# One core's decoder stack: five edits at the start of the attention, in its block order, at its end and in the first FFN block

## The reference, cut to what matters

```python
x = x + layernorm(attention(layernorm(x), Wqkv, Wo))      # 32 heads of 16, one shared key and value head,
                                                          # causal, slope * (k - q) added to the scores
x = x + layernorm(ffn(layernorm(x), 4-bit gate/up/down))  # h = silu(x @ Wg) * (x @ Wu);  out = h @ Wd, width 1376
x = x + layernorm(block-masked linear(layernorm(x)))
x = x + layernorm(linear + low-rank Fourier update(layernorm(x)))
# dequantisation: W[k, n] = scale[group(k), n] * (code[k, n] - (zero[group(k), n] + 1))
```

## Time and profile before

| | |
|---|---|
| three runs, median (lowest, highest) | 1154.56 us (1153.49, 1155.82) |
| the profiled execution | 1155.38 us |
| its span on the core | 1153.6 us |
| TensorE busy | 1095.1 us (95%) |
| VectorE, ScalarE, GpSimd busy | 717.3, 624.1, 423.1 us |
| mean granted TensorE clock | 0.986 |

### The profile page before, as it was taken

How to read it: one execution, slowest core, us unless ns; L and a number is a source line. 1 busy time by engine, 2 the same in 40 slices (tenths; PEclk the granted TensorE clock), 3 DMA queues, 4 the chain that set the end, 5 groups by cost and what they waited for, 6 DMA issues and landing times.

```text
span 1153.6 us, 16292 instructions
## 1 busy us (share of the span) xinstructions
PE 1095.1 (95%) x5822; PEld 678.7 (59%) x5888; DVE 717.3 (62%) x1675; ACT 624.1 (54%) x1067; POOL 423.1 (37%) x494
## 2 busy tenths in 40 slices
PE   7699999999999999899998899999999999999997
PEld 7445346345334334334535667788878878777885
DVE  6597997996999999799622644251141151247674
ACT  5265875766778689987794434211111111136775
POOL 4364252354210634322265655221121121124765
PEclk8799999999999999999999999999999999999999
DMA  6416104003213012101310221330030032211101
GB/s 184 131 43 166 29 20 119 21 20 77 62 38 101 22 35 64 58 29 47 95 37 28 75 64 39 110 110 1 1 110 1 1 79 101 74 37 74 37 37 74
DMA packets 66349, 70.62 MB, mean 61 GB/s; under 512 B 39854, under 2 KB 45510, under 8 KB 64708
## 3 DMA queue, kind: packets, MB, share of 16 engines
q1 hardware_dynamic: 62540, 59.82, 17.4%
q0 software_dynamic: 3152, 8.63, 2.3%
q10 hardware_dynamic: 576, 1.11, 0.3%
HBM read 50.27 MB, written 18.87 MB: 60 GB/s over the span
## 4 chain that ended last, share of the span: by engine, by line
PE 78%; DVE 11%; ACT 5%; issue 2%; POOL 2%; DMA 1%; SPq 1%; POOLq 0%; DVEq 0%; ACTq 0%
PE PO L1511 10%; PE ST L1497 8%; PE bank L1413 8%; PE f_pair L61 7%; PE f_pair L63 7%; PE f_pair L62 7%; DVE bank L1207 3%; PE f_Y L1906 3%; PE f_Y L1908 3%; PE f_Y L1907 3%; ACT PT L1119 3%; PE l_psum L2331 2%; PE l_psum L2333 2%; PE l_psum L2332 2%; DVE mx L1209 2%
## 5 line engine op out<-in xcount | busy, mean ns | idle before, releaser
L1119 ACT ACTIVATE PT<-ST,lowered 128x512 f32<-128x512 f32 x576 | 355.1, 693 | 72.6 <-PE PO L1511 31.7
L1207 DVE CUSTOM_DVE_ANT_0 bank<-bank,tail_mask 128x512 f32<-128x512 f32 x320 | 211.1, 719 | 21.2 <-PE bank L1413 20.9
L1413 PE MATMUL bank<-KS,QS 125*128 125x512 bf16 (+2 forms) x896 | 179.4, 307 | 10.2 <-DMA QS<-q_scratch 4.7
L1497 PE MATMUL ST<-QS,KS 128*128 128x512 bf16 x523 | 170.2, 384 | 11.0 <-ACT PT L1119 4.3
L1209 DVE TENSOR_REDUCE mx<-bank 128x2 f32<-128x512 f32 (+2 forms) x256 | 161.1, 681 | 25.9 <-PE bank L1413 11.4
L1037 POOL TENSOR_SCALAR_AFFINE_SELECT PT<-PT 128x512 f32<-128x512 f32 x128 | 79.2, 646 | 220.3 <-ACT PT L1119 219.7
L1511 PE MATMUL PO<-PT,V 128*32 128x512 f32 x1152 | 152.6, 604 | 2.9 <-ACT OT L1132 1.7
L1832 DVE TENSOR_TENSOR f_h<-f_h,f_pair 128x512 f32<-128x512 f32 (+1 forms) x44 | 30.2, 687 | 194.8 <-ACT f_h L1776 194.8
L1776 ACT ACTIVATE f_h<-f_pair 128x512 f32<-128x512 f32 (+1 forms) x44 | 26.3, 598 | 217.1 <-PE f_pair L63 217.1
L1736 POOL TENSOR_TENSOR f_h_part<-f_h,f_h_part 128x512 fp32r<-128x512 f32 (+1 forms) x44 | 56.7, 1289 | 232.0 <-ACT f_h_part L1780 232.0
L61 PE MATMUL f_pair<-f_xT,gw 128*128 128x512 f32 (+1 forms) x352 | 139.9, 398 | 0.0
(11 more groups left out here) (210 smaller groups left out, 1799.0 us busy)
## 6 DMA issues: line engine op xcount, KB each, us to landing
QS<-q_scratch SPq DMA_DIRECT2D x96, 128.0 KB
q_scratch<-QP SPq DMA_DIRECT2D x36, 128.0 KB, 1.9
xres<-_attn_hidden_states_dram POOLq DMA_DIRECT2D x16, 256.0 KB, 3.3
x_dram<-xout POOLq DMA_DIRECT2D x16, 256.0 KB, 2.4
xin<-x_dram SPq DMA_DIRECT2D x4, 1024.0 KB, 7.7
f_xsum<-x_dram SPq DMA_DIRECT2D x4, 1024.0 KB, 7.0
x_dram<-f_xsum SPq DMA_DIRECT2D x4, 1024.0 KB, 4.7
out_dram<-l_xout SPq DMA_DIRECT2D x7, 512.0 KB, 2.8
```

What stands on the lines that cost most here:

```text
L1119: act.activation(PT[:, quad % PT_RING, n % 4, :], ST[:, n % ST_RING, :], ACT.Exp, bias=lowered[:, 0:1]).then_inc(p_done, 1)
L1207: v.tensor_tensor_reduce(at(u), at(u), tail_mask[:, :], 1.0, -3e38, ALU.add, ALU.max, mx[:, i % 2, z, h:h + 1]).then_inc(bank_free_dve, 1)
L1413: last = pe.matmul(at(u)[:, j * w:(j + 1) * w], QS[0:ROWS1, slot, h + j, :], KS[b][0:ROWS1, k0:k0 + w], start=(j == 0 or not diag), stop=( ...
L1497: pe.matmul(ST[:, n % ST_RING, :], KS[b][0:ROWS2, kb * P:(kb + 1) * P], QS[0:ROWS2, slot, h:h + 4, :], start=True, stop=True).then_inc(st_ ...
```

## The change

1. **Start.** `WARM_UP` is 13, and five more idle products (`WARM_TURN`) stand on TensorE after the transposes of the first rows. GpSimd waits for VectorE's first weight part before it does its last. The query writes go to DRAM for two m at once (runs of 256 elements; half as many DMAs, twice the size), and the sets of one part are written to `QS` in one DMA that reads its source several times (three DMAs of 48, 32 and 16 rows rather than six of 16). The rows of the sets and `gmask` are renumbered, and the inner layout of `QP` changes with them. The planner's costs for these DMAs change, and the hand-written order of SyncE's queue as well.
2. **Block order.** The second sequence's blocks run 7, 6, 5, 4, 2, 1, 0, 3 rather than 7 to 0.
3. **First gate and up tile.** Its 24 products leave the FFN and become eight steps (`ff`) of the attention's plan; they go into two banks of `ST`, whose release is one semaphore, `first_full`.
4. **Pieces.** `between(n)` replaces `pieces_during`: one piece after each gate, up and down group, none back to back, with a wait of its own for each piece on TensorE. ScalarE takes silu between a piece's copy and its high part.
5. **Statistics of block 1.** One tile for each n rather than four at once.

```diff
-WARM_UP = 12
+WARM_UP, WARM_TURN = 13, 5
-def pieces_during(n):
+def between(n):
+    extras = [("dq", j) for j, (u, _) in enumerate(DQ) if UNITS[u][0] > 0] + [("xt", t) for t in range(4)]
+    return extras[max(0, 3 * n - 2):3 * n + 1]
-BLOCKS = [(0, qb) for qb in range(QB)] + [(1, qb) for qb in reversed(range(QB))]
+BLOCKS = [(0, qb) for qb in range(QB)] + [(1, qb) for qb in (7, 6, 5, 4, 2, 1, 0, 3)]
+FF_STEPS = 2 * DC
-    took = {"dt": 440, ..., "at": 440, "wo": 1400}
+    took = {"dt": 440, ..., "at": 440, "wo": 1400, "ff": 690}
-            t = max(t, *(end["qout", piece_of(i), m] for m in range(4)))
-            end["stacked", i] = max(t + 4500, end.get(("stacked", i - 1), 0) + 3000)
-            free["sp"] = t + 1500
+            t = max(t, *(end["qout", piece_of(i), m] for m in (1, 3)))
+            end["stacked", i] = max(t + 3500, end.get(("stacked", i - 1), 0) + 2500)
+            free["sp"] = t + 1800
+        if at["ff"] < FF_STEPS and at["tile"] == 4 * QUADS:
+            m = at["ff"] // DC
+            made = [("dl", j) for j in EARLY_PIECES if UNITS[DQ[j][0]][1] <= m]
+            out.append((known(("read", 4 * QUADS - 1), ("xt", AFTER, 3), *made), free["pe"] + 9000, ("ff", at["ff"])))
-                for g in range(SETS):
-                    if Q_PART[g] == part:
-                        sp.dma_start(QS[g:SETS * HD:SETS, slot, :, :].rearrange("d h q -> d (h q)"),
-                                     q_scratch[b, qb, part].rearrange("d h m q -> d (h m q)")).then_inc(qs_in[slot], 16)
+                n, r = PART_SETS[part], PART_ROW[part]
+                sp.dma_start(QS[r:r + n * HD, slot, :, :].rearrange("d h q -> d (h q)"),
+                             q_scratch[b, qb, part].rearrange("d h m q -> d (h m q)").unsqueeze(1).to_broadcast([HD, n, NH * P])).then_inc(qs_in[slot], 16)
-            for m, part in ((0, 0), (1, 0), (0, 1), (0, 2), (2, 0), (1, 1), (1, 2), (3, 0), (2, 1), (2, 2), (3, 1)):
+            for m, part in ((1, 0), (1, 1), (1, 2), (3, 0), (3, 1)):
+            pool.wait_ge(wx_lo, 1)
             weights_low(DC - 1)
+            def first_tile(x):
+                m, c = divmod(x, DC)
+                if x == 0:
+                    freed(pe, ("xt", AFTER, 3))
+                    pe.wait_ge(p_done, 4 * QUADS)
+                if c == 0:
+                    pe.wait_ge(dq.w_lo, pieces_before(0, m))
+                out = ST[:, m, :]
+                pe.matmul(out, hi(dq.gw[0][:, 0, m, c, 0:P]), hi(xT[0][:, c, :]), start=(c == 0), stop=False)
+                ...
+                if x == FF_STEPS - 1:
+                    last.then_inc(first_full, 1)
             for u in FIRST:
                 fill(u)
+                if u == ("xt", 0, 1):
+                    idle_products(WARM_TURN)
+            silu(0, 0)
+            h_high(0, 0)
+            piece_or_rows(between(0)[0])
+            for n in range(1, NT):
+                x = between(n)
+                piece_or_rows(x[0])
+                piece_or_rows(x[1], then=n)
+                h_high(0, n)
+                piece_or_rows(x[2])
```

More of the change, by code:

```diff
@@ L37 @@
 SETS = len(Q_PART)
+PART_SETS = [Q_PART.count(part) for part in range(PARTS)]
+PART_ROW = [HD * Q_PART.index(part) for part in range(PARTS)]
 POS = slice(SETS * HD, SETS * HD + 2 * PARTS)
@@ L55, in hi @@
     return ap.bitcast(F32R)
-def three_pass(pe, out, w_hi, w_lo, x_hi, x_lo, chunks):
-    for c in range(chunks):
-        pe.matmul(out, w_hi(c), x_hi(c), start=(c == 0), stop=False)
-        pe.matmul(out, w_hi(c), x_lo(c), start=False, stop=False)
-        last = pe.matmul(out, w_lo(c), x_hi(c), start=False, stop=(c == chunks - 1))
-    return last
 INTER = 1376
@@ L352, in commit_pe @@
         name = u[:-1] if kind in STEPPED else u
-        if kind not in ("tile", "pv") and (kind not in STEPPED or u[-1] == 0):
+        if kind not in ("tile", "pv", "ff") and (kind not in STEPPED or u[-1] == 0):
             bank_of.append(name)
@@ L613, in uses_in_order @@
             (begun if u[-1] == 0 else ended).append(u[:-1])
-        elif u[0] not in ("tile", "pv"):
+        elif u[0] not in ("tile", "pv", "ff"):
             begun.append(u)
@@ L1567, in pair_uses @@
         for kind, n in ffn_events(blk):
-            if kind in ("dq", "gate", "xt") + NEXT:
+            if kind in ("dq", "gate", "xt") + NEXT and (kind, blk, n) != FIRST_GATE:
                 use = (kind, blk + 1, n) if kind == "xt" else (kind, blk, n)
@@ L1762, in weight_high, with silu @@
                 act.activation(hi(weights(0, j)), product(j), ACT.Copy).then_inc(w_hi, 1)
-            for blk in range(FB):
+            def silu(blk, n):
+                w, s, g = tile_w(n), slot(blk, n), blk * NT + n
+                if g:
+                    act.wait_ge(pair_full, g)
+                else:
+                    act.wait_ge(att.first_full, 1)
+                if g >= 2:
+                    act.wait_ge(h_lo, g - 1)
+                act.activation(h[0:w, s, :], banks(("gate", blk, n))[0:w, 0, :], ACT.Silu).then_inc(sil_done, 1)
@@ new lines, in h_high, with piece_or_rows @@
+            def h_high(blk, n):
+                w, s, g = tile_w(n), slot(blk, n), blk * NT + n
+                act.wait_ge(h_ready, g + 1)
+                if g >= 2:
+                    act.wait_ge(down_done, g - 1)
+                act.activation(hi(h_parts[0][0:w, s, :]), h[0:w, s, :], ACT.Copy).then_inc(h_hi, 1)
+            def piece_or_rows(x, then=None):
+                kind, n = x
+                if kind == "dq":
+                    weight_copy(n)
+                else:
+                    xt_hi(1, n)
+                if then:
+                    silu(0, then)
+                if kind == "dq":
+                    weight_high(n)
```

171 lines of the change are left out of this document (105 added, 66 removed).

## The result

The changed kernel takes 1145.01 us (median of four runs, 1144.14 to 1145.92). The kernel before took 1154.03 us beside it (1153.04 to 1155.82). The ratio is 0.9919, with a 95% interval from 0.9907 to 0.9932: 9.0 us faster where 24.8 were forecast. The direction was right, and the time lies 4 us outside the range. In the profiled execution (1145.92 us) the span is 1144.2 us, 9.4 less than before.

What follows compares the result with a forecast made beforehand. TensorE was busy 1095.1 of 1153.6 us, leaving 58.5 us idle plus half-clock losses to win. 11.6 + 5.7 + 7.5 = 24.8 off the profiled 1155.38 gave 1130.6, by the median 1129.8, written 1130; range 1125 to 1141.

Steps and rivals of the forecast that it cites:

- Start: Start of the kernel: shorter waits for queries and maxima and a clock that stays up, -11.6 us in sum.
- (b): Start: last query write issued at about 22.6 us, old landing and stack times kept, first scores 5.4 us earlier.
- (d): Start: three stack issues, not six, ahead of the maxima's DMAs; wait -1.5 us, clock behind it another -2.0.
- (a): Start: five more idle products keep the clock up for the first products; -2.2 us, contained in the 5.4.
- its 1 us: Start: query writes in 512 B runs might land about 1 us sooner; left out of the sum.
- (c): Start: after a wait of only about 1.4 us the clock stays up behind the first scores, -2.7 us.
- The second rival: Start: stack wait bound by transfers, twice the landing; +2.9 us, clock +2.7, maxima's wait stays; 1136 to 1138; 9%.
- Attention's end: End of the attention: moved gate and up products fill TensorE's waits, less a cost for block order; -5.7 us.
- The gain of 5.0 + 1.7: Attention's end: about 5.0 us of idle time filled, and 1.6 to 1.7 from output products at full clock.
- The order's 1.0 us: Attention's end: 1.0 us set against the gain for the new block order; the last block's stack and maxima counted as covered.
- FFN block 0: First FFN block: spread pieces take 5.8 of 7.0 us of waits, 1.2 left, and the clock gains; -7.5 us.
- The 1.7 us for the clock: FFN block 0: without waits of 2 us, the 7.00 us at 0.76 from 665 us give back 1.7.

Runs made afterwards that it cites:

- e2_last: The change with the last query write of piece 0 issued ahead of the first stack DMA rather than behind it: 1144.62 us.
- f4_write_alone: The change with the last write ahead of all stacks, the queue waiting for its landing, and the residual loads late: 1143.77 us.
- e6_six_late_order: The change with six stack DMAs, residual loads after the second piece's low parts, and the second sequence's blocks in order 7 to 0: 1142.79 us.
- e3_single: The change with each query write again for one m (runs of 128 elements, twice as many DMAs): 1146.12 us.
- e11_max_first: The change with the maxima of block 0 issued ahead of the stack of block 2 rather than behind it: 1141.30 us.
- e10_ff_last_order: The change with blocks in order 7 to 0 and the 24 gate and up products behind the last output product: 1147.11 us.
- f3_before_max: The kernel before with only the maxima of block 0 ahead of the stack of block 2 and the residual loads late: 1148.75 us.
- e13_grouped: The change with block 1's row statistics and normalisation in groups again, as before the change: 1146.06 us.

## Why the prediction was right or wrong

**Start: forecast -11.6 us, measured -0.1 in the two profiles, and -3 at most in other executions of the same code.** What failed is the landing times, taken over from the old schedule, of the last write and the first stack (b) and of the maxima (d).

- (a) was right: the products from 13.3 us on ran at full clock. The five idle products took 2.3 us for the 3.0 forecast, the real ones began at 12.69 us, and GpSimd's last two low parts of the first piece start at 20.54 us for 23.27. The shift reached SyncE's queue.
- (b) failed in the sentence "I take 2.85, for the total of bytes is the same and the last write no longer lies behind eleven others", and in the 2.49 us for the stack behind it. The issue time was right. From this issue to the first scores 5.34 us were forecast and 33.21 - 22.63 = 10.6 measured, of which the write's landing took 7.7. The write is not the root of it: landed in 1.8 us (e2_last) or 2.0 (f4_write_alone), the first scores still came at 33.23 and 31.17 us, for then the stack took the time. The bytes are the same, but they now want the transfer engines in less time, and 512 KB of residual loads fall among them. With these loads moved away the first scores came at 29.5 to 31.2 us. The wait forecast at 1.4 us was 3.44 us at the least (e6_six_late_order). The Trainium skill, "DMA: Bandwidth & Descriptors", section "Specifications", gives 512 B as the least transfer for line rate. By it runs of 512 B should land no later than shorter ones; that did not show in the landings of the last write: 4.6 and 5.0 us with runs of 256 B (e3_single), and 5.2 to 7.7 with 512 B in the seven profiles with the change's start and its loads. Leaving its 1 us out was right.
- (c) fell with (b): after 7.15 us of idle time the clock fell, 0.61 in the stretch.
- (d) failed in the same way. The three issues did take 2.35 us rather than 4.62, and the maxima then queued for 5.5 us behind the bytes of these three. e11_max_first put a price of 2.5 to 3.7 us on that place in the queue.

The second rival, "bound by the transfers", named the mechanism. Its price of 6 to 8 us and its 9% were too low; I had bounded the landing at twice its old value without asking what the engines' share would be. The share that I quoted, 0.65, is that of a stretch behind the wait. Ahead of it the trace of the kernel before already had full engines, on the old schedule:

```profile
26.00:28.00 2.00, 2.00 (x19) 2.00 (x18) 0.58 (x2) 2.00 (x2) 0.00 (x0) 1.00 1.01 263
```

With the start at nothing, the same sum gives 1141.6, and with the sizes measured below, 4.0 and 5.4, it gives 1141.6 + 1.7 + 2.1 = 1145.4, for 1145.0 measured.

**Attention's end: forecast -5.7, measured -4.0**, for both edits together (e10_ff_last_order against the change; taken singly, 4.7 for the products less 0.9 for the order). The mechanism was right: no idle time and full clock from 612 us on. The gain of 5.0 + 1.7 was over-sized, for a part of the waits moves to the FFN's head. In e10_ff_last_order, with the products there, TensorE waits for nothing over 0.3 us between the output products and 690 us. In the change it waits 1.07 us for the second piece and 0.67 for the first `h` part:

```profile
635.55 0.39 PE L668 MATMUL f_pair<-f_xsum,identb 128*128 128x512 bf16 x1 [1.07 <-DVE d_wf L1874]
...
640.47 0.50 PE L2012 MATMUL f_Y<-dw,f_h_part 128*128 128x512 f32 x1 [0.67 <-POOL f_h_part L1780]
```

The order's 1.0 us was near the measured 0.9, partly by luck: the cost is there only where the clock falls, and its reason is one that I had counted as covered, the slot's release and then 5 us to the first pass for a landing of 2.49.

**FFN block 0: forecast -7.5, measured -5.4 against the profile before and -8.0 against that of f3_before_max.** The pieces' waits fell from 7.0 to 1.4 us in the change (forecast 1.2), and to 0.4 in e10_ff_last_order. Missing is a term of the other sign: in block 0 the waits for GpSimd's parts at the down products are 1.5 us in the change and 0.8 in e10, for none before, and two waits of 0.37 and 0.32 us at about 690 us are new. All waits of the block together fell by 5.5 us in e10. The 1.7 us for the clock does not show in the 5.4, since e10 ran longer at half clock at the attention's end than the kernel before did. The first row is e10's, the second the kernel before's:

```profile
623.00:629.00 6.00, 5.97 (x14) 4.74 (x15) 0.00 (x0) 0.48 (x1) 1.91 (x2) 0.50 0.13 46
625.80:631.80 6.00, 5.83 (x19) 4.28 (x21) 0.66 (x1) 1.20 (x2) 1.97 (x3) 0.72 0.11 44
```

At 0.50 these 6 us lose 3.0, at 0.72 they lose 1.7. Without this difference of 1.3 the FFN would have gained about 6.7 us, and the attention's end only about 2.7; both are estimates from these two rows. The total doesn't depend on the split. The mechanism that I gave for the waits was wrong as well: of the three old waits one was a pair of pieces, and one was the grouped statistics (1.3 us by e13_grouped), which I had priced at nothing.

## What to carry to other kernels

When a queue's backlog is taken away, its transfers come closer together: read the share of the transfer engines in that stretch before using an old landing time for the new schedule. In front of a wait that ends on a small DMA, look at what large DMA was issued just ahead of it; here one swap in the queue gave about 3 us, and with the residual loads late about 6 us on the old kernel as well. A landing that ends a chain need not be its cause: when an experiment shortens it, look whether what waits for it comes sooner, and look up which DMA a largest landing belongs to. When work is moved to fill a gap, ask what it had been covering where it came from. When two profiles are compared by stage, put the granted clock behind each wait beside them; here it alone made 1.4 and 2.6 us between stretches of the same code.

## What the runs showed of the hardware that I had not expected

- In these two runs a write's landing depended on what its queue had issued ahead of it, and not on what came right behind it. In e2_last a write of 128 KB landed in 1.8 us with six stack DMAs (1.5 MB) behind it, and the next write, behind these six, in 10.0; in f4_write_alone it was 2.0 and 7.6.
- The maxima's 8 KB landed in 5.5 us behind 768 KB and in 1.8 us ahead of them.
- The bytes moved while the engines' share was about 1.0 varied from 119 to 367 GB/s from one microsecond to the next (119 after, at 27 us; 367 before, at 27 us). The stack's form doesn't explain this, and it stays open.
- The clock at the start: after five idle products without a gap it stayed at 1.00 in this profile, where 2.82 us of idle time had brought 0.50 before.
- The clock behind a wait is not the same in every execution: after 3.14 us it stayed at 1.00 in the kernel before and was 0.57 over the next 4 us in f3_before_max; after 2.59 us it was 0.59 in the change, and 1.00 after 2.47 us in e3_single.
